# Taking a step's first neighbour maximum ahead of the end of attention in a two-layer graph network on one core

## The reference

```python
def layer0(A, X, W, b):                    # X = relu(layernorm(x))
    vals, idx = top_k(where(A != 0, -arange(N), -inf), 25)
    feats = X[idx]                         # 25 gathered rows for each node
    agg = feats.max(axis=2)                # (with 0 in it where the degree is <= 25)
    return relu(concat([X, agg]) @ W + b)  # x = x + this

def layer1(X, mask, W, a, bias):           # X = relu(layernorm(x))
    hidden = X @ W.T
    attn = leaky_relu(a1[:, :, None] + a2[:, None, :])
    attn = softmax(where(mask > 0, attn, attn - 1e12))
    return attn @ hidden + bias            # x = x + this
```

## Time and profile before

| what | before |
|---|---|
| median of three timed runs | 6101.06 us (6094.42 to 6102.2) |
| profiled execution: its time | 6146.83 us |
| profiled execution: span of the core | 6145.0 us |
| mean granted clock of TensorE, share of full speed | 0.667 |
| PE busy | 2712.3 us (44%) |
| DVE busy | 2613.4 us (43%) |
| ACT busy | 1564.8 us (25%) |
| POOL busy | 3058.5 us (50%) |
| DMA, mean over the span | 132 GB/s |
| chain that ended last, largest shares | another core or an unknown queue 35%, DVE 23%, PE 17%, issue 12% |

### The profile page before, as it was taken

The page is one execution under the profiler, slowest core; times in us unless marked ns, Lnnn a source line. Parts: engine busy times, 40 slices in busy tenths (PEclk is TensorE's granted clock), DMA queues, the critical chain, the costliest instruction groups (busy, mean ns, idle before and its releaser), DMA issues.

```text
span 6145.0 us, 39084 instructions
## 1 busy us (share of the span) xinstructions
PE 2712.3 (44%) x10078; PEld 1696.3 (28%) x10078; DVE 2613.4 (43%) x6725; ACT 1564.8 (25%) x1745; POOL 3058.5 (50%) x3204
## 2 busy tenths in 40 slices
PE   1222244344444444444444435444354444444369
PEld 0111122232222323222332323222232232322246
DVE  4444434354343543344533435334353344453342
ACT  3111122222222222222322223222222222222234
POOL 5566545544454545545454554445544464554430
PEclk6555566666666666666666656666566666667689
DMA  6444433443334433344433344333443344443330
GB/s 252 131 140 131 141 116 125 150 145 120 115 127 148 148 120 121 126 141 157 135 132 115 126 155 143 119 119 123 153 143 121 115 133 140 147 144 117 103 108 25
DMA packets 228389, 809.23 MB, mean 132 GB/s; under 512 B 59466, under 2 KB 60372, under 8 KB 207828
## 3 DMA queue, kind: packets, MB, share of 16 engines
q0 software_dynamic: 153600, 419.64, 22.4%
q1 hardware_dynamic: 56308, 321.91, 14.3%
q10 hardware_dynamic: 18432, 67.12, 2.7%
HBM read 690.98 MB, written 119.54 MB: 132 GB/s over the span
## 4 chain that ended last, share of the span: by engine, by line
another core or an unknown queue 35%; DVE 23%; PE 17%; issue 12%; ACT 9%; DVEq 2%; POOL 1%; DMA 0%; ACTq 0%; SPq 0%; POOLq 0%
DVE highest L854 10%; PE acc L1262 7%; ACT nm_t L510 4%; DVE lin L878 3%; PE bank L1203 2%; ACT wgt L546 2%; DVEq L894 2%; PE acc L1226 1%; DVE stat L715 1%; PE bank L1220 1%; ACT pen L540 1%; PE bank L1183 1%; PE pen L1254 1%; DVE top L788 1%
## 5 line engine op out<-in xcount | busy, mean ns | idle before, releaser
L465 POOL DMA_INDIRECT near<-table_dram,idx x3200 | 3058.3, 956 | 2853.0 <-DVE agg L859 1653.9
L1262 PE MATMUL acc<-hid,wgt 128*128 (+1 forms) x4096 | 1216.3, 450 | 1270.3 <-ACT wgt L546 979.5
L1262 PEld LDWEIGHTS acc<-hid,wgt 128*128 128x128 f32 x4096 | 881.8, 226 | 1451.2 <-issue 1200.5
L854 DVE TENSOR_TENSOR highest<-near,highest 128x512 f32<-128x512 f32 x1280 | 889.8, 695 | 173.4 <-DVE highest L854 92.5
L546 ACT ACTIVATE wgt<-pen,a_slope 128x512 f32<-128x512 f32 x448 | 303.0, 682 | 1808.7 <-remote 1288.5
L1203 PE MATMUL bank<-w_sb,h_t 128*128 128x256 f32 x1024 | 413.4, 573 | 792.3 <-ACT h_t L631 722.4
L870 DVE SCALAR_TENSOR_TENSOR x_q<-bank,x_q 128x256 f32<-128x256 f32 x128 | 53.9, 421 | 1255.5 <-PE bank L1205 1077.6
L1203 PEld LDWEIGHTS bank<-w_sb,h_t 128*128 128x128 f32 x1024 | 280.8, 288 | 884.3 <-ACT h_t L631 753.5
L510 ACT ACTIVATE nm_t<-adj_i,big_c 128x2048 bf16<-128x2048 int32 x128 | 499.5, 3953 | 4.4 <-DMA adj_i<-in_adj_dram 4.4
L788 DVE MAX8 top<-key 128x8 f32<-128x256 f32 (+1 forms) x1024 | 360.6, 387 | 299.5 <-remote 180.6
L631 ACT ACTIVATE h_t<-bank 128x512 f32<-128x512 f32 x128 | 75.9, 593 | 1491.5 <-remote 785.4
(11 more groups left out here) (144 smaller groups left out, 2312.6 us busy)
## 6 DMA issues: line engine op xcount, KB each, us to landing
adj_i<-in_adj_dram SPq DMA_DIRECT2D x128, 1024.0 KB
nmask_dram<-nm_t ACTq DMA_DIRECT2D x128, 512.0 KB
nm_q<-nmask_dram SPq DMA_DIRECT2D x29, 2048.0 KB
near<-table_dram,idx POOLq DMA_INDIRECT x3200
h_q<-table_dram SPq DMA_DIRECT2D x32, 512.0 KB
x_q<-in_x_dram SPq DMA_DIRECT2D x32, 512.0 KB
xmid_dram<-x_q SPq DMA_DIRECT2D x32, 512.0 KB
o_q<-xmid_dram SPq DMA_DIRECT2D x32, 512.0 KB
```

Source lines behind the costliest of these rows:

```text
L465: pool.indirect_dma_start(out=near[:, t % 2, k, :], out_offset=None, in_=table, in_offset=bass.IndirectOffsetOnAxis(ap=idx[:, t, k:k + 1], ...
L854: nc.vector.tensor_tensor(highest[:, :], pair(k), highest[:, :], ALU.max).then_inc(mx_step, 1)
L1262: mm = nc.tensor.matmul(acc[:, t, 0:C + 1], wgt_part(j)[:, t * P:(t + 1) * P], hid[:, bass.ds(batch * NJ + j, 1), 0:C + 1].rearrange("p a ...
```

## The change

DVE's order is changed in three places. In a step, `gathered(0)`, the call of max(s,0), is taken away from the step's head. The step now takes max(s+1,0) near its end, behind the last residual and the last index search, and ahead of `attend_end` and of the statistics. The max(0,0) of the first step is taken before the loop, and `last_quad` no longer takes max(31,0), since step 30 has. No instruction is added or removed, and no other engine's order changes.

```diff
@@ last_quad
-                maximum(LAST, 0)
                 for u in range(2):
                     dve.wait_ge(nm_out[u], 16 * 2 * QUADS)
@@ step
-                gathered(0)
                 if "attend" in stages:
                     attend_setup(a, lo)
                 finished(0)
@@ step
                 else:
                     finished(3)
+                if "gather" in stages:
+                    maximum(s + 1, 0)
                 if "attend" in stages:
                     attend_end(a)
                 if "gather" in stages:
@@ ahead of the loop
             dve.wait_ge(zero_out, 16 * (TRING // QB))
+            maximum(0, 0)
             schedule(dve, step)
```

## The result

The changed kernel takes **6735.85 us** (median of four runs, 6717.41 to 6741.47); the kernel before takes 6097.74 us on the same chip (four runs, 6088.54 to 6102.2). The ratio is **1.1043**, with a 95% interval of 1.1018 to 1.1069. The forecast was 6622 us, with a range of 6270 to 6760. The profiled execution after is that of 6717.41 us.

The account below looks back on a forecast made before the run. Waits, with PE's signals late during gathers, were taken to bound the kernel. +25.3 - 6.0 = +19.3 us for each of 27 ends of attention, 521 us, put on the median of 6101.06 gave 6622 us; range 6270 to 6760.

Parts of the forecast that it names:

- What bounds the kernel: Whole kernel: waits set the time, and PE's signals arriving late during gathers matter more than POOL's wait for a maximum.
- The maximum itself costs nothing in either place: DVE's max(s,0): hidden in its old and new place; up to 14.1 us a step if the cover were gone.
- The end of attention, +25.3 us: Attention's last tiles: without POOL's 28.88 us pause, late signals delay its end by 25.3 us; bounds 0 and +34.
- What comes sooner, -6.0 us: After attention: undisturbed max(s,1) lets the gather (s,3) start 6.0 us sooner after the end of attention; bounds 0 and 6.
- The rest of the period unchanged: From the gather (s,3) on: the following gathers depend on indices and maxima as before, so no change.
- the short pause tips over: Rival, pause before the gather (s+1,0): 22 more periods pass the threshold and save 10.8 us each; 6384 us, chance 0.25.
- The sum: 27 ends of attention at +19.3 us, 521 us; the four steps without attention at 0, 30 us either side.
- The signs: Profile after: 28.88 us pause gone, 62 us issue, pause of 50 or more, weights 17 us apart, periods near 209 us.
- No difference: Rival: both places of the maximum are hidden and the earlier gather only waits longer for max(s,1); 6101 us, chance 0.05.
- faster: Rival: attention ends in time, leaving only the gain of 6.0 us in 27 steps; 5939 us, chance 0.10.
- the port lock: Rival: the maximum's thirteen DVE operations hold POOL off for 8.4 us a step more; 6849 us, chance 0.02.
- The delay on the projection: Rival: attention is in time, but the projection's handoffs fall into the gather (s,2), +13 us; 6290 us, chance 0.11.

Follow-up runs that it names:

- the hold: Changed kernel, with POOL holding the gather (s,2) until the end of attention of the step before is signalled; 6254.58 us against 6111.4, ratio 1.0255, with late signals.
- two slower cases: Changed kernel with POOL holding the gather (s,2) for the end of attention (ratio 1.0255), or for the projection's scores (ratio 1.0610), each against the kernel before.
- one faster one: Kernel before, with POOL holding the gather (s+1,0) in all periods until PE's penalty signal of tile 4 arrives; 5879.0 us against 6100.56, ratio 0.9608.
- the first experiment: Changed kernel, POOL holding the gather (s,2) until the end of attention, on a chip without late signals; 4265.14 us against 4266.7, ratio 0.9996.
- narrow rows: Changed kernel with each gathered row cut to its first quarter, 256 B instead of 1 KB, computing other data in layer 0; 6730.3 us in one run.
- three kernels that moved such pauses away: The changed kernel (ratio 1.1043), and it with the gather (s,2) held for the projection's scores (1.0610) or for the end of attention (1.0255).
- the kernel held for the projection: Changed kernel, POOL holding the gather (s,2) of steps 4 to 30 until ACT has copied the projection's scores; 6485.82 us against 6100.56, ratio 1.0610.

## Why the prediction was right, point by point

*What bounds the kernel.* That waits for late signals of PE do, and not POOL's wait for a maximum, held: the maximum came earlier, and the kernel lost 10.4%.

*The maximum itself costs nothing in either place.* Held. It ends 54.9 us ahead of the end of attention, which was idle time of DVE, and behind the statistics the setup still waits for the projection (17.73 us, ended by ACT's copy).

*The end of attention, +25.3 us (bounds 0 and +34).* This is the term that carried the forecast. Its mechanism held, and it was mis-sized. The end of attention fell 43.5 us behind the end of G(s,1) and not 10.7: **+32.8 us**, near the upper bound (40.6 to 44.9 us behind in all 27 steps; +32.5 in the mean). I had let each tile come through under a gather at the 17.7 us of the earlier trace rows. Tile 14 took 32.9 us behind tile 13 (3234.51 to 3267.43), and tile 15 came 17.5 behind that, only after the gathers. The catching up took 7.6 us, as the 8.2 us of step 30 had it, and not 4.2. The bound with those 8.2 us was the better reading, since step 30 was the one stretch of before that had 50 gather instructions in a row.

*What comes sooner, -6.0 us.* G(s,3) starts 48.7 us behind the end of attention (3338.14 - 3289.48), and was 55.8 in the earlier trace rows. In the mean of the 26 periods it is 49.0 us for 55.3: **-6.3 us**.

*The rest of the period unchanged.* This step failed in part. It was the rival "the short pause tips over", priced at -10.8 us for each period that tips. It came true in 12 more periods: 16 of 26 are of the short kind, where it was 4. The pause in the rows above is 4.87 us and the next one 15.24. The mean period went from 189.3 to 210.1 us, **+20.8**, where I had +19.3. It is near the forecast because two misses nearly cancel: +7.2 of the first term, and -5.4 of the third, for which 12 x 10.8 / 26 would give -5.0. That is luck. With the first two terms as measured and no more pauses tipped, the sum is 27 x (32.5 - 6.3) = 707 us and the time 6808 us, outside the range, which ended at +25 a period though the first term alone had a bound of +34. What tipped the pauses stays open; the cause that the prediction named for it, later index words, is not shown.

*The sum.* 26 periods gave +540.8 us. The last quad gave -34.3: from the last of the 27 ends of attention to the end of the span it took 319.4 us, now 285.1. I had no term for that, and its cause stays open. The steps up to the first end of attention, set at 0 with 30 to either side, gave +64.1: 29.9 of it the first end of attention itself (41.1 us behind a gather, where it was 11.2), and 34.1 in the steps ahead of it, outside the 30 that I had allowed. The waits there point at the projection: ACT waits 19.03, 19.26 and 19.34 us with no known releaser for its products (L535) at 454.02, 620.56 and 787.17, the first some 3.5 us behind the end of a gather that was issued from 419.49 on. Before, its five waits ahead of L535 up to there came to 23.9 us in sum, ended by PE. Together 570.6 us in the profiled executions, and 638 us between the medians; the profile of before stood 0.75% above its median, that of after 0.3% below. Of the miss of 114 us, 50 are the sum and the rest lies in where those profiled executions stood.

*The signs.* The pause before G(s,2) gone, one issue of 62 us, a pause of over 50 behind it, weights 17.5 us apart, max(s,1) at 8.9 us and periods of 210 us all came. ACT's waits with no known releaser grew by 1110 us, and not by some 675.

*The rivals.* No difference and faster are refuted by the ratio. So is the port lock: gather instructions last 955 ns in the mean, no longer than before. The delay on the projection did not appear in the loop, but it did in the first steps, and in full when the hold restored the end of attention (14.8 us, priced at 13).

*What is shown and what is argued.* Shown: the late signals belong to the gathers (in the kernel before, none of the 159 penalties that PE ended over 6 us behind a gather and ahead of the next left ACT idle for over 0.1 us), do not depend on their bytes, and follow POOL's pauses when these are moved by a wait on POOL alone (two slower cases, one faster one). Argued only: why they are late. The Trainium skill, page "NOTIFIC — the notification-queue block", section "7.1 Overflow: three behaviours, one of which stalls the engine", says that the block which writes records of events can hold back the engines that produce them. No run here separates that from another shared path, and none shows why chips differ.

The record has more on this than the experiments used. The two semaphores on which the gathers report are due 51,200 updates, 16 for each of 3200 instructions. The trace of the first experiment, without late signals, has 51,083 of them; that of the kernel before has 7,461, and that with narrow rows 7,549. PE's penalty semaphore has 512 of 512 updates in the first, and 474 in the second. So where signals are late, most updates of the gathers are missing from the trace too. That fits a path for semaphore updates, or for the records of them, that the gathers' updates fill, and it is the rival that I left untested: a gather with fewer updates. Every execution here comes with a span and a granted clock that were recorded with it, so no run shows whether the late signals, and the difference between chips, would be there without the recording.

## What to carry to other kernels

Before moving a wait away, ask what ran in its shadow on the *other* engines: here POOL's pauses let chains of signals catch up (attention, projection, layer 0), and the three kernels that moved such pauses away lost 638, 385 and 143 us. When a wait has no known releaser, look at which engine is issuing DMAs just then, and how long after it stops the wait ends. And time a kernel on more than one chip before tuning it by its waits, without a recorder if that can be had: 30% of the time (6098 against 4267 us) was there on some chips and not on others.

## What the hardware showed that was not expected

- The same kernel before took 6032 to 6150 us on some chips, and 4267 and 4278 us on two others. A handoff from PE to ACT during a gather takes 0.09 us without late signals, and up to 44.7 us with them (54.0 in the kernel held for the projection).
- With late signals there is a threshold in POOL's pause. In the kernel before, pauses of 3.1 to 3.8 us ahead of G(s+1,0) were followed by one of 27.4 to 28.4 us, and pauses of 4.2 to 5.2 us by one of 15.5 to 16.6 us. In the kernel after, 3.92 us sufficed (15.60 behind it) and 3.42 did not (27.06). A wait that lengthened it by 1.5 us took 12.5 us off the next.
- A wait added to the issuing engine made the kernel 3.9% faster (ratio 0.9608).
- The traces themselves differ: that of the kernel before holds 18,223 semaphore updates in all, that of the first experiment, with nearly the same instructions, 68,544.
- A gather instruction of 128 rows takes 951 ns in the mean with rows of 256 bytes, and 955 with rows of 1 KB.
